# A four-layer gated cross-attention model on one core: the opening and closing steps of the top-k stages moved to the neighbouring blocks' other lanes

## What is computed

```python
for L in range(4):
    x = x + tanh(g_xattn[L]) * xattn_L(layernorm(x), ctx)
    x = x + tanh(g_ffn[L]) * ffn_L(layernorm(x))
# xattn: 0 performer (causal linear attention, 16 heads)
#        1 wide: 8 heads of 64, softmax over the 64 largest scores of each row
#        2 plain softmax, 16 heads of 8
#        3 16 heads of 8, softmax over the 32 largest scores of each row
# ffn:   0 attention + top-2 of 8 linear experts   1 gated experts (top-2 of 8 + shared)
#        2 GELU experts (top-2 of 8 + shared)      3 attention over a gated mix of 16 experts
```

## Time and profile before

| | us |
|---|---|
| median of three runs | 2522.1 |
| profiled execution | 2522.9 |
| its span, first to last instruction | 2521.1 |
| setup | 18.0 |
| block 1, Chunk0 alone | 99.1 |
| ORDER_FIRST, once | 132.3 |
| 1_2, four times | 148.2 to 148.3 |
| 3_2, four times | 154.3 to 154.4 |
| 3_0, three times | 148.0 |
| 1_0, three times | 143.2 |
| ORDER_LAST, once | 118.9 |
| Chunk4 alone | 68.4 |

### The profile page before, as it was taken

The page is one execution under the profiler, slowest core; times in us unless marked ns, Lnnn a source line. Parts: engine busy times, 40 slices in busy tenths (PEclk is TensorE's granted clock), DMA queues, the critical chain, the costliest instruction groups (busy, mean ns, idle before and its releaser), DMA issues. The chain is left out here.

```text
span 2521.1 us, 41407 instructions
## 1 busy us (share of the span) xinstructions
PE 2116.8 (84%) x12585; PEld 1644.6 (65%) x12585; DVE 2049.1 (81%) x8036; ACT 1388.3 (55%) x3341; POOL 909.3 (36%) x1400
## 2 busy tenths in 40 slices
PE   5878888888989889887989988788998988888676
PEld 3555666676758668666867667666776766757455
DVE  1399996958989896977989898795899989696981
ACT  2435565675645456685544557576554545667431
POOL 4142213327462222426435221333636321242432
PEclk9889899999999999999999989999999989999787
DMA  2000100010000100001000100001000010000100
GB/s 105 7 1 11 67 1 1 1 74 1 1 9 1 78 1 1 1 1 74 1 9 1 78 1 1 1 1 74 2 9 1 1 78 1 1 1 1 67 3 3
DMA packets 9917, 48.71 MB, mean 19 GB/s; under 512 B 738, under 2 KB 7906, under 8 KB 8162
## 3 DMA queue, kind: packets, MB, share of 16 engines
q1 hardware_dynamic: 9698, 46.07, 4.7%
HBM read 45.02 MB, written 1.05 MB: 18 GB/s over the span
## 5 line engine op out<-in xcount | busy, mean ns | idle before, releaser
L185 DVE MATCH_REPLACE8 workQ<-top_eight,workQ 128x256 f32<-128x256 f32 x1664 | 667.4, 408 | 0.0
L187 DVE MAX8 top_eight<-workQ 128x8 f32<-128x256 f32 x1664 | 617.9, 413 | 0.4
L221 POOL TENSOR_TENSOR att_pQ<-att_pQ,top_rest 128x512 f32<-128x512 f32 x192 | 245.6, 1279 | 270.2 <-ACT top_rest L214 269.8
L687 PE MATMUL bank<-workP 128*128 128x256 f32 x1024 | 280.9, 399 | 30.1 <-ACT att_pP L817 26.2
L817 ACT ACTIVATE att_pP<-bank,att_nmaxP 128x256 f32<-128x256 f32 x512 | 216.3, 481 | 80.1 <-DVE att_nmaxP L866 76.3
L687 PEld LDWEIGHTS bank<-workP 128*128 128x128 f32 x1024 | 180.9, 195 | 89.4 <-issue 62.4
L839 POOL TENSOR_SCALAR workP<-workP,const 128x256 f32<-128x256 f32 x256 | 125.3, 493 | 254.9 <-PE bank L687 188.4
L193 POOL TENSOR_SCALAR att_nmaxQ<-top_lead 128x2 f32<-128x2 f32 x192 | 36.8, 192 | 472.8 <-DVE top_lead L187 472.1
L866 DVE TENSOR_REDUCE att_nmaxP<-bank 128x2 f32<-128x512 f32 x256 | 172.7, 680 | 25.0 <-PE bank L687 24.3
L473 PE MATMUL bank<-workQ 128*128 128x256 f32 x512 | 146.6, 413 | 42.3 <-ACT att_pQ L204 31.0
L187 DVE MAX8 top_lead<-bank 128x8 f32<-128x256 f32 x384 | 144.9, 419 | 43.0 <-PE bank L473 28.7
(11 more groups left out here) (302 smaller groups left out, 4613.6 us busy)
## 6 DMA issues: line engine op xcount, KB each, us to landing
expert_w<-in_pack3w SPq DMA_DIRECT2D x4, 4608.0 KB, 13.7
expert_w<-in_pack4w SPq DMA_DIRECT2D x4, 4096.0 KB, 13.2
pack<-in_pack SPq DMA_DIRECT2D x1, 2266.0 KB, 11.4
pack<-in_pack SPq DMA_DIRECT2D x1, 1028.0 KB, 7.7
mix_wb<-in_ctx SPq DMA_DIRECT2D x1, 1024.0 KB, 5.0
x_in<-in_x SPq DMA_DIRECT2D x8, 128.0 KB, 2.1
ctx_tok<-in_ctx SPq DMA_DIRECT2D x8, 128.0 KB, 2.3
ctxT<-in_ctxT SPq DMA_DIRECT2D x8, 128.0 KB, 2.6
```

Of the source, the lines that this page charges most:

```text
L185: ins = nc.vector.match_replace(self.work[:, u % 2, j, :], eight, src, GONE)
L187: ins = nc.vector.max(eight, src)
L221: self.k.nc.gpsimd.tensor_tensor(v, v, self.rest[:, :, :], ALU.subtract).then_inc(self.p_ready, 1)
L687: mm = self.k.nc.tensor.matmul(self.banks[u % 2][:, j * T:(j + 1) * T], self.q1[:, u % self.RING, j * P:(j + 1) * P], self.kT, start=True, ...
```

## The change

The two top-k classes are cut in three each. WideTop and HeadsTop keep lane Q's rounds: they have one step ahead of the first round, which issues the first scores, and no closing steps. WideStart and HeadsStart (three steps each: layer norm, projections, and the ones and zeros beside v by POOL memsets, which the setup did before) stand at the end of lane P in the block before: WideStart behind LinearExperts, HeadsStart behind GeluExperts. WideEnd (three steps) stands at the beginning of lane P in the block after, ahead of GatedExperts; HeadsEnd (five steps) at the beginning of lane M, ahead of MixedAttention, in one bank. What passes between blocks lies in two TopSet tiles (k, q, v) and one TopSpace (o). There are three x tiles instead of two, so the wait for the old store goes. WeightedSum's part tile now lies in P's workspace. The six order strings are new. The number of blocks, what each batch goes through and the arithmetic stay the same; the first block ends with a WideStart, and the lone Chunk4 at the end begins with a HeadsEnd.

```diff
-class WideAttention(TopSelect):
+class WideStart(Units):
+    def pe(self, pe, s):
+        if s == 0:
+            self.before.wait_banks(pe)
...
+        if s == 1:
             for j in range(NT):
                 pe.wait_ge(self.proj_copied, j + 1)
                 nc.tensor.matmul(b[2 + j][:, :], self.ctxT[:, j * P:(j + 1) * P], w["wv1"], start=True,
                                  stop=True).then_inc(self.proj, 1)
+            self.ln.pe(pe)
...
+class WideTop(TopSelect):
+        self.units(1, H1, self.topk // 8, 9, 0)
+    def act(self, act, s):
...
+            if u == 0 and self.before is not None:
+                act.wait_ge(self.before.back, NT)
...
+class WideEnd(Units):
+    def act(self, act, s):
+        if s == 0:
+            for j in range(NT):
+                act.wait_ge(self.back, j + 1)
+                self.k.nc.scalar.activation(self.otT[:, j, :, :], self.banks[j][:, :], ACT.Copy).then_inc(self.otT_ready, 1)
+    def dve(self, dve, s):
         if s == 2:
             dve.wait_ge(self.out_ps, 1)
...
-            if self.before is not None:
-                dve.wait_ge(self.before.stored, 16)
...
-        self.stages = [Performer(k, "P", k.x_in, self.ctxT, k.ctx_tok, b, self.load), att,
-                       LinearExperts(k, "P", k.x_in, k.x[lane], att, b, 4, old)]
+        linear = LinearExperts(k, "P", k.x_in, x, att, b, 4)
+        self.stages = [Performer(k, "P", k.x_in, self.ctxT, k.ctx_tok, b, self.load), att, linear,
+                       WideStart(k, "P", x, self.ctxT, b, k.tops[i % 2], linear, weights)]
...
+        self.end = HeadsEnd(k, "M", 3, k.x[i % 3], k.psum[7], 3)
+        self.stages = [self.end, self.mix]
...
+        self.end = WideEnd(k, "P", x, b, 1)
+        self.stages = [self.end, gated, PlainHeads(k, "P", 2, x, ctxT, b, "b", gate=2, before=gated), gelu,
+                       HeadsStart(k, "P", 3, x, ctxT, b, k.tops[i % 2], gelu)]
```

More of the change, by code:

```diff
@@ L917, in pe @@
         if s == 0:
+            if self.weights is not None:
+                pe.wait_ge(self.weights, 16)
+            self.before.wait_banks(pe)
             for c in range(4):
@@ new lines, in pool, with dve, __init__, score @@
+    def pool(self, pool, s):
+        if s == 0:
+            self.k.nc.gpsimd.memset(self.tops.wide_v[:, :, :, HD1:], 1.0).then_inc(self.padded, 1)
+            self.ln.pool(pool)
+            pool.wait_ge(self.padded, 1)
+    def dve(self, dve, s):
+        if s == 0:
+            self.ln.dve_stats(dve)
+        if s == 1:
+            self.ln.dve_scale(dve)
+class WideTop(TopSelect):
+    topk = 64
+    def __init__(self, k, banks, tops, before):
+        self.name = "wide"
+        self.k, self.banks, self.tops, self.before = k, banks, tops, before
+        buf = TopSpace(k)
+        self.p, self.pT, self.o = buf.p, buf.pT, buf.o
+        self.nmax = k.sb("top_nmax", [P, H, NT])
+        self.rden = k.sb("wide_rden", [P, H1, NT])
+        n = "top_"
+        self.scores, self.max_ready, self.exp_done = k.sem(n + "scores"), k.sem(n + "max"), k.sem(n + "exp")
+        self.p_ready, self.pT_ps, self.pT_copied = k.sem(n + "p"), k.sem(n + "pT_ps"), k.sem(n + "pT")
+        self.pv_done, self.rden_ready, self.o_ready = k.sem(n + "pv"), k.sem(n + "rden"), k.sem(n + "o")
+        self.top_buffers(k, buf, n)
+        self.units(1, H1, self.topk // 8, 9, 0)
+    def score(self, pe, u):
+        c, a = divmod(u, 2)
+        r = slice(HD1 * a, HD1 * (a + 1))
+        if u >= self.ring:
+            pe.wait_ge(self.exp_done, u - self.ring + 1)
+        for j in range(NT):
+            mm = self.k.nc.tensor.matmul(self.banks[u % 2][:, j * T:(j + 1) * T], self.tops.qT[r, c, j * P:(j + 1) * P],
+                                         self.tops.kT[r, c, :], start=True, stop=True)
+        mm.then_inc(self.scores, 1)
+    def pe(self, pe, s):
+        nc, b = self.k.nc, self.banks
+        if s == 0:
@@ L1355, in __init__, with wait_banks @@
         self.units(3, self.N, 2, 4, 1)
+    def wait_banks(self, pe):
+        pe.wait_ge(self.hT_ready, self.N * FF2)
+        pe.wait_ge(self.sum.taken, E8 + 1)
     def pe(self, pe, s):
@@ L1774, with __init__ @@
 class Chunk3(Chunk):
-    def __init__(self, k, lane, top_banks):
-        self.stages = [HeadAttention(k, "Q", 3, k.x[lane], k.ctxT[lane], top_banks, "a", 32, 3)]
+    def __init__(self, k, i, top_banks, before):
+        self.stages = [HeadsTop(k, 3, top_banks, k.tops[i % 2], 32, before)]
 def interleaved(chunks, order):
```

493 lines of the change are left out of this document (247 added, 246 removed).

## The result

The changed kernel takes 2578.7 us (median of 4 runs, 2575.3 to 2582.1), the kernel before, on the same chip, 2522.4 (2521.3 to 2523.6): ratio 1.0223, 95% interval 1.0205 to 1.0241. Forecast were 2550 and a range of 2475 to 2590. So the sign and the range held, and the loss of 56 us is twice the 28 that I had summed. The profiled run took 2575.3 us, the fastest of the four, with a span of 2573.5.

The account below looks back on a forecast made before the run. Neither TensorE nor VectorE was taken to bind alone; lane P paces the second half of 1_2 and 3_2 blocks. Changes per block kind summed to +28.4 us on 2522.1, giving 2550 us, range 2475 to 2590.

Parts of the forecast that it names:

- The ends: Block 1 gains a wide opening (+6.9 us) and the lone M block a heads closing (+6.5), with nothing beside them.
- the rival with VectorE as the bound: VectorE stays the bound and P keeps up: faster, 2440 us; chance 0.30 together with its half-way case.
- if VectorE doesn't wait in the heads stage: Sign of being wrong, for 1_2 blocks: VectorE was forecast to wait some 10 us in P's plain heads.
- (a): Block start to first scores of P's plain heads: 49.2 us in 1_2 (before 40.5), 44.5 in 3_2 (37.8).
- (b): P's plain heads, limited by PE: 38.8 us in 1_2 (before 46.2), 42.8 in 3_2 (52.8).
- (c): P's closing, layer norm and router: 12.0 us in 1_2 (before 13.1), 13.0 in 3_2.
- (d): The GELU experts, PE-bound: 43.1 us in 1_2 (before 44.1), 47.6 in 3_2.
- (e): Block tail: x added, heads opening, barrier; 8.1 us in 1_2 (before 4.4) and in 3_2 (before 3.6).
- PE overfull: Rival: the six 3_0 and 1_0 blocks lose 3 to 6 us more each, up to 2586 us; chance 0.14.
- Q's last head is not late: End of 1_2: Q's last head drains beside the GELU experts and the block's tail, adding no time.
- Q's closing no longer disturbs the linear experts: In 3_0 and 1_0 blocks: moving Q's closing away saves the linear experts about 1 us.
- the opening's idle 4 us: Last block: this idle time goes, M's closing work comes in, last round ends at 107 us; block -3.5.

Follow-up runs that it names:

- e2: The changed kernel without the wide closing at the front of lane P in the eight 1_2 and 3_2 blocks: 2570.6 us.
- e3: The changed kernel with unread products on PE ahead of the gated experts (14), the GELU experts (6) and in the heads opening (4): 2567.8 us.
- e1: The changed kernel without the heads opening at the end of lane P in the eight 1_2 and 3_2 blocks: 2571.6 us.
- e13: The changed kernel with the subtraction for Q's last head in 1_2 and 3_2 blocks done by VectorE instead of GpSimd: 2574.9 us.
- e5: The changed kernel with all six order strings searched anew in a small block model, steps and work the same: 2570.4 us.
- e11: The changed kernel with e5's searched strings for the 1_2, first shared and last blocks, its own for the others: 2557.8 us.
- e8: The changed kernel with only the openings moved to lane P, closings done by Q as before, orders searched: 2518.9 us.
- e9: The changed kernel with only the narrow heads opening moved to lane P, wide opening and both closings back in Q, searched orders: 2487.3 us.
- e4: The kernel before the change with 6 unread products on PE ahead of its GELU experts: 2514.1 us.
- e10: e9 with 6 unread products on PE ahead of the GELU experts and 4 in the narrow opening: 2505.2 us.

## Why the prediction was right in sign and half in size

**What held.** The ends: +6.8 and +7.2 for 6.9 and 6.5. P as the pacing lane: 1_2 and 3_2 got longer though VectorE's first selection starts 7 to 10 us sooner; the rival with VectorE as the bound (2440) is out. The closing and router stretch took 12.1 for 12.0, with VectorE busy 9.6 for 10. The drain of the last block took 6.3 for 6.5. The shares of the whole span (TensorE 84%, VectorE 81%) did not tell which engine paces: stages with different bounds alternate here. The projections at half clock, which the upper bound of 9 us allowed for, did not come in block 1, where from 117.1 to 124.0 us the clock was 1.00; the lone block's closing ran at 0.50 up to its x (2497.7 to 2504.7), not only "in part at the lower clock". The store that I called long finished had landed only 1.4 to 2.1 us before the x of the linear experts that waited for it in 3_0 and 1_0, but VectorE never sat idle for it.

**What was right by luck.** I had the heads stage at 38.8 because PE would be 98% busy and VectorE 75%. It is 38.3 with both at 92%, since 17 rounds ran beside it and not 14. My own sign of being wrong, "if VectorE doesn't wait in the heads stage", nearly came: it waits 3.0 us in six pieces. VectorE's idle time went elsewhere.

The 3_2 block is luck too: +7.4 us for four, forecast 6.4, from parts that missed and cancelled. The block from 1014.8, cut at the same places:

```profile
1014.80:1063.60 48.80, 37.89 (x174) 30.35 (x174) 39.68 (x156) 20.53 (x56) 15.02 (x25) 0.79 0.00 1
1063.60:1105.10 41.50, 39.47 (x256) 28.11 (x256) 41.10 (x146) 33.53 (x81) 17.15 (x33) 1.00 0.01 1
1105.10:1117.50 12.40, 8.25 (x54) 6.21 (x53) 12.23 (x54) 5.75 (x15) 5.12 (x8) 0.97 0.01 1
1117.50:1159.80 42.30, 41.43 (x267) 36.20 (x267) 29.20 (x128) 37.66 (x82) 10.88 (x18) 0.97 0.00 1
1159.80:1170.20 10.40, 4.71 (x30) 3.08 (x30) 2.93 (x8) 4.98 (x13) 4.58 (x6) 1.00 0.00 0
```

Against the forecast (a) is 4.3 us longer (44.5), (b) 1.3 and (c) 0.6 shorter, (d) 5.3 shorter (47.6) and (e) 2.3 longer (8.1). The two steps that fail in 1_2, (a) and (e), fail here as well, and a GELU stage booked too long covers them.

The rival "PE overfull" ends nearest to the measured time (2568 to 2586) and is not what happened: the six 3_0 and 1_0 blocks lie 9 us above my forecast together, where it asked for 18 to 36, and in 3_0 they lie below it.

**1_2, (a): 51.5 us, forecast 49.2.** VectorE's work was a little over-counted (busy 45.4, my sum 47.1; 22.5 rounds ran, not 24). Mis-sized was the last term, 1.0 us of small gaps: VectorE idles 6.1 us up to there, where my sum had 2.1; 3.8 of it lie in the gated stage, mostly in waits for P's small steps, 0.5 to 0.8 us at a time. e2 shows that the closing is not the cause, e3 that the clock is not (50.7 us with it at 0.83 instead of 0.57).

**1_2, (d) and the sentence "Q's last head is not late".** (d) came out 1.8 us shorter than forecast, but behind it Q was late: no row of mine looked for a wait of VectorE inside the GELU stage, and there is one of 4.1 us with seven rounds behind it, which did harm for the first time in the new order. The last selection ends at 141, so Q's drain ends with P's opening, not ahead of it (e1), and meets P's tail on ScalarE and GpSimd.

**1_2, (e): x 3.9 us after the last GELU product, forecast 2.0.** About 1.0 of the 1.9 is the hold that e13 takes away; the rest fits the copy behind the table load, which was read, not tested. After x the 4.5 us for the opening held: 4.6 to the last instruction.

Together (a) and (e) are 4.3 us, less 1.8 in (d) and 0.5 in (b): +2.1 to +2.3 in three blocks and 4.5 in the one of 155.7. e5 and e11 show that 5.8 us of each block were the order's: I had taken the new order as given, counted rounds up to each cut, and not asked what else stands in it.

**1_0: +10.1 for three, forecast -2.1.** One of them is 3.2 us longer than its twins. Its first 10 us, then the twin's:

```profile
710.50:720.50 10.00, 8.28 (x26) 6.07 (x27) 7.19 (x31) 1.11 (x3) 1.82 (x4) 0.51 0.14 41
1318.80:1328.80 10.00, 7.47 (x31) 5.65 (x32) 8.55 (x36) 1.11 (x3) 1.82 (x4) 0.83 0.14 41
```

The granted clock is 0.51 there and 0.83 in the twin; how much of the 3.2 us that makes was not taken apart. In the twins the failing step is "Q's closing no longer disturbs the linear experts (about 1)": from the last selection to x it now takes 11.0 us (9.8 before), so this step adds 1.2 us where I had taken 1 off, 2.2 of the 3.0 us that a twin missed by, because M's attended products, one of 0.67 before in that place, are now two, 0.68 and

```profile
1446.74 1.77 DVE L1698 TENSOR_TENSOR mix_z<-mix_wb,mix_rest 128x512 f32<-128x512 f32 x1
```

M runs later, since its own closing now stands ahead of it. This is read from the trace, no run isolates it. What a wide opening behind x costs depends on the order. In e8 against e9 it is +4.9 us in each 3_0, by the same order but for its own three letters, and +5.5 in each 1_0, where I had let 5 us of VectorE's gain pay for most of it. In the changed kernel's own order a 3_0 block carries the opening, and M the closing, at 148.2 us, 0.2 more than before.

**Last: +0.1, forecast -3.5.** Before, Q's opening was not idle time of VectorE: in the first 10.4 us M's router ran in it.

```profile
2333.60:2344.00 10.40, 7.95 (x24) 5.41 (x24) 6.92 (x36) 4.46 (x12) 3.13 (x5) 0.54 0.90 363
```

After the change that work stands between the selections, which then last 108.6 us with 4.0 of waits:

```profile
2381.30:2489.90 108.60, 78.45 (x418) 59.12 (x417) 104.60 (x425) 44.41 (x106) 46.03 (x63) 0.82 0.08 35
2489.90:2497.70 7.80, 2.86 (x12) 1.10 (x12) 0.50 (x2) 1.89 (x4) 1.26 (x1) 0.66 0.06 17
```

I had booked "the opening's idle 4 us" as gone and no wait inside: the last round ends at 111.1, forecast 107.

**Still open.** Why closings and openings together cost more than apart, 25 us by e5 and 12 by e11, was not taken apart further than by blocks (in e5 the eight 1_2 and 3_2 blocks carry 23 us of it, 3.3 and 2.4 in each), and no order is known to be the best for its kernel. The spread between runs and twin blocks goes with the granted clock (0.922 in the changed kernel's run of 2575.3 us, 0.916 in that of 2582.1; 0.89 in the 1_2 block of 153.3 us, 0.87 in that of 155.7), but what sets it off in one block and not in its twin was not found.

## What to carry to other kernels

Idle time at one lane's edges is not yet time to be won: here the 25 us that VectorE idled in a 1_2 block moved behind the lane that paces and stayed, 27 us of them. Nor can the price of a moved step be read off its length: 4.5 us behind P's x saved 0.1 to 0.8 us a block when left out again (e1), and in e9 the same opening in the same place goes with a gain. Price each part by itself, with orders made for it: here one quarter of the change gains 22 us and the other three lose 70 to 83. And read a new hand-written order for each in-order engine, instruction by instruction, for waits with long work queued behind them, before counting what stands ahead of a milestone.

## What the runs showed of the hardware

Three VectorE instructions with their tensors in SBUF lasted longer when a GpSimd tensor_tensor of 1.27 us had started just ahead of them: 1.47 us for 0.48 (the sum x), 1.28 for 0.34 (the scale), 1.77 for 0.68 (M's products). MAX8 and MATCH_REPLACE8 did not, though their work tile lies in SBUF too (0.43 us at most in the changed kernel). With products that nobody reads the granted clock was higher (1.00 for 0.76 in e4; 0.83 for 0.57, 0.93 for 0.85 and 1.00 for 0.88 in e3), and the kernel before took 8 us less; in e10 the kernel took 18 us more with them, some 10 of these at the end of blocks where the clock was 1.00 without them. Eight products of the GELU experts took 3.76 us at a clock of 0.50 and 1.99 at 1.00.
